# Second gathers during the last expert pass, and rows of the last pass chosen on TensorE, in a fused transformer block

## The reference

```
t = rmsnorm(h)                           # 1024 tokens x 256
probs = softmax(t @ gate_w)              # 8 experts
topw, topi = top_k(probs, 2), topw /= sum(topw)
out_e(t) = (relu(t @ w1[e]) * (t @ w3[e])) @ w2[e]      # hidden width 1024
y = h + sum over the two chosen experts of topw * out_e(t)
result = x + gb * y                      # gb: one row of 256 for each batch
```

## Time and profile before

| | |
|---|---|
| three timed runs, us | 1058.65, 1061.76, 1062.86 (median 1061.76) |
| profiled execution, first to last instruction, us | 1063.1 |
| PE busy | 965.1 us (91%) |
| DVE busy | 789.4 us (74%) |
| ACT busy | 753.5 us (71%) |
| POOL busy | 466.7 us (44%) |
| mean granted TensorE clock | 0.962 |

### The profile page before, as it was taken

The page is one execution under the profiler, slowest core; times in us unless marked ns, Lnnn a source line. Parts: engine busy times, 40 slices in busy tenths (PEclk is TensorE's granted clock), DMA queues, the critical chain, the costliest instruction groups (busy, mean ns, idle before and its releaser), DMA issues.

```text
span 1063.1 us, 22951 instructions
## 1 busy us (share of the span) xinstructions
PE 965.1 (91%) x6862; PEld 901.5 (85%) x6862; DVE 789.4 (74%) x2308; ACT 753.5 (71%) x2122; POOL 466.7 (44%) x550
## 2 busy tenths in 40 slices
PE   5589999999899899999999999999998589999991
PEld 3379899998789799988999999999887489999991
DVE  6779998989899577777777777777764756666646
ACT  3368788887888688788888778877884346555641
POOL 4346668777656333433444332232222852222243
PEclk8899999999999899999999999999997699999996
DMA  8799879787476675465557455354303365555313
GB/s 178 185 233 274 208 190 276 209 213 201 112 177 147 167 190 155 122 164 135 136 140 166 122 168 120 110 153 126 71 1 120 115 221 172 166 170 162 103 58 116
DMA packets 146059, 166.18 MB, mean 156 GB/s; under 512 B 79194, under 2 KB 100714, under 8 KB 140816
## 3 DMA queue, kind: packets, MB, share of 16 engines
q1 hardware_dynamic: 129440, 143.58, 52.0%
q0 software_dynamic: 3712, 11.16, 3.3%
q10 hardware_dynamic: 12784, 9.97, 3.0%
HBM read 105.88 MB, written 58.79 MB: 155 GB/s over the span
## 4 chain that ended last, share of the span: by engine, by line
PE 56%; DVE 17%; issue 10%; ACT 9%; DMA 4%; POOL 1%; SPq 1%; DVEq 0%; ACTq 0%; POOLq 0%
PE psO L1086 14%; PE psS L1053 10%; PE psX L1063 8%; PE psY L1102 6%; PE psP L985 6%; ACT wgt_hi L1319 3%; DVE pbuf L1734 2%; DVE gated L2074 2%; DVE pTl L1756 2%; PE psO L1069 2%; PE psS L1236 2%; PE psP L998 2%; ACT relu_s L1624 2%; PE psX L1236 1%; DVE den L1748 1%
## 5 line engine op out<-in xcount | busy, mean ns | idle before, releaser
L1351 ACT ACTIVATE pbuf<-pbuf,nmax 128x256 f32<-128x256 f32 (+3 forms) x512 | 264.9, 519 | 45.8 <-DVE nmax L1734 44.7
L1053 PE MATMUL psS<-kT,qE 128*128 128x256 f32 (+3 forms) x1024 | 238.2, 317 | 25.7 <-DVE nmax L1734 24.1
L1734 DVE CUSTOM_DVE_ANT_0 pbuf<-psS,mcau 128x256 f32<-128x256 f32 (+3 forms) x512 | 219.9, 435 | 46.9 <-PE psS L1053 41.0
L1756 DVE TENSOR_TENSOR pTl<-psX,pTh 128x512 fp32r<-128x512 f32 x272 | 187.1, 688 | 73.5 <-ACT pTh L1319 72.9
L1319 ACT ACTIVATE pTh<-psX 128x512 fp32r<-128x512 f32 x272 | 160.7, 591 | 55.7 <-PE psO L1086 39.3
L1053 PEld LDWEIGHTS psS<-kT,qE 128*128 128x128 f32 x1024 | 160.2, 192 | 40.3 <-DVE nmax L1734 33.7
L1086 PE MATMUL psO<-pTh,vpad 128*128 128x256 f32 x1088 | 187.1, 294 | 3.2 <-DVE oS L1762 2.0
L798 POOL TENSOR_TENSOR ol<-oS,oh 128x256 fp32r<-128x256 f32 x128 | 94.8, 741 | 200.7 <-ACT oh L1319 196.2
L1063 PE MATMUL psX<-idn,pbuf 128*128 128x128 f32 x1088 | 162.2, 274 | 3.1 <-DVE pTl L1756 3.1
L1086 PEld LDWEIGHTS psO<-pTh,vpad 128*128 128x128 f32 x1088 | 150.3, 190 | 10.5 <-DVE oS L1762 5.4
L1063 PEld LDWEIGHTS psX<-idn,pbuf 128*128 128x128 f32 x1088 | 126.5, 141 | 9.4 <-DVE pTl L1756 3.3
(11 more groups left out here) (295 smaller groups left out, 2369.0 us busy)
## 6 DMA issues: line engine op xcount, KB each, us to landing
qd<-st SPq DMA_DIRECT2D x32, 1024.0 KB, 4.5
qE<-qd SPq DMA_DIRECT2D x128, 256.0 KB, 6.0
mrawV<-in_w_moe SPq DMA_DIRECT2D x32, 384.0 KB
mrawB<-in_w_moe SPq DMA_DIRECT2D x32, 384.0 KB
kT<-kd SPq DMA_DIRECT2D x64, 128.0 KB, 4.4
kT<-kd SPq DMA_DIRECT2D x32, 256.0 KB, 4.3
kd<-st SPq DMA_DIRECT2D x7, 1024.0 KB, 4.8
xg<-sq ACTq DMA_DIRECT2D x7, 640.0 KB, 6.1
```

The costliest lines, as they stand in the source:

```text
L1053: last = mm(psS[j % 2][:, 0:n], qE[:, g % 2, j, t * P:(t + 1) * P], kT[:, g % 2, c, k0:k0 + n], start=(c == 0), stop=(c == 1))
L1351: nc.scalar.activation(pj, pj, ACT.Exp, bias=nmax[:, u % 4, j:j + 1], scale=-1.0, accum_out=sums[:, u % 4, j:j + 1]).then_inc(a_exp, 1)
L1734: V.tensor_tensor_reduce(probs(u, j), psS[j % 2][:, 0:n], mcau[:, SEQ - n:], -SCALE, 3e38, ALU.add, ALU.min, nmax[:, u % 4, j:j + 1]).then ...
L1756: V.tensor_tensor(pTl[:, kt % 2, :], psX[kt % 2][:, :], pTh[:, kt % 2, :], ALU.subtract).then_inc(v_pl, 1)
```

## The change

- The second gathers follow the first ones at once, without waiting for the last pass; the first ones no longer wait for m_gate. A row of `yg` that belongs to the last pass is still zero then. The last pass's output isn't stored to DRAM any more.
- Instead, the last output is kept in SBUF, split in `yh` and `yl`, and for each pair of token tiles TensorE multiplies it with `chooser`, a matrix of zeros and ones of 3 x 128 slots by 1024 tokens: 12 matmuls of 256 columns a pair, 48 in all.
- `chooser` is made by ACT in the last pass, in chunks 1 to 6: relu(1 - (slot - row)^2), two activations of 512 columns a piece, from the tokens' higher slots spread over all partitions. Those come through DRAM: SP stores them (1024 values of 4 bytes, behind the loads of expert 1) and loads them back, spread, ahead of the last pass.
- DVE works out `known` = x part + first rows times share and gate in chunks 4 to 7 of the last pass. POOL works out gate times yN, xN plus that, and `scale2` = gate times second share, two tiles at the start of each of experts 2 to 5.
- Tail: per pair of tiles DVE adds product and second rows, multiplies by `scale2`, and adds `known` for pairs 0 and 2; POOL does that add for pairs 1 and 3. SP stores pairs.
- The last load of `xin` goes from POOL to SP; the flags of `shares` go to tiles of their own (`lesser`, `part`), so that `order` stays.

```diff
@@ -711,6 +738,10 @@
                 if e == 1:
                     sp.wait_ge(s_x, 1)
                 load_expert(e, range(NPC))
+                if e == 1:
+                    sp.wait_ge(v_slot, 2)
+                    sp.dma_start(second_slots.rearrange("(t p) -> p t", p=P), order[:, 1, :],
+                                 allow_slow_non_contiguous=True).then_inc(st_slot, 16)
 
             def leave(i):
...
@@ -719,12 +750,25 @@
                     .then_inc(st_z, 16)
                 sp.dma_start(yg[bass.ds(i * TP + 2 * P, TP - 2 * P), :], ysb[XT * P - TP:P, 2, :]).then_inc(st_z, 16)
 
-            experts(sp, lambda e, first: None, lambda e, i, j, ahead: leave(i), range(NE - 1, NE))
-            leave(first_pass_of(sp, NE))
-            for t in range(NT):
-                sp.wait_ge(v_out, t + 1)
-                sp.dma_start(out[t // TB, t % TB * P:(t % TB + 1) * P, :], xN[:, t, :]).then_inc(st_res, 16)
-            sp.wait_ge(st_res, 16 * NT)
+            def leave_and_load(e, i, j, ahead):
+                leave(i)
+                sp.wait_ge(s_x, i + 2)
+                sp.dma_start(xin[:, :, :], xg[bass.ds((i + 2) * TP, XT * P), :].rearrange("(j p) d -> p j d", p=P))\
+                    .then_inc(st_slot, 16)
+
+            def load_slots(e, first):
+                sp.wait_ge(st_slot, 16)
+                sp.wait_ge(w_hi, NPC * first + NPC - 1)
+                sp.wait_ge(w_lo, 6 * first + 6)
+                sp.dma_start(slot_rows, second_slots.partition_broadcast(P)).then_inc(ld_slot, 16)
+
+            experts(sp, load_slots, leave_and_load, range(NE - 1, NE))
+            for n in range(NT // 2):
+                sp.wait_ge(g_out, n // 2 + 1) if n % 2 else sp.wait_ge(v_out, n // 2 + 1)
+                at = n % 2 * 2 * P
+                sp.dma_start(out[n // 2, at:at + 2 * P, :].rearrange("(t p) d -> p t d", p=P), xN[:, 2 * n:2 * n + 2, :])\
+                    .then_inc(st_res, 16)
+            sp.wait_ge(st_res, 16 * NT // 2)
 
...
+            def begin(e, first):
+                apart(pool)
+                if e == 2:
+                    pool.wait_ge(v_share, 1)
+                    pool.wait_ge(v_ye, 4 * TB)
+                if 2 <= e < 2 + NT // 2:
+                    for t in (2 * e - 4, 2 * e - 3):
+                        link(G.tensor_tensor(yN[:, t, :], yN[:, t, :], GB[:, t // TB, :], ALU.mult))
+                        link(G.tensor_tensor(xN[:, t, :], xN[:, t, :], yN[:, t, :], ALU.add))
+                        link(G.tensor_scalar(scale2[:, t, :], GB[:, t // TB, :], share[:, 1, t:t + 1], None, ALU.mult))
+
+            experts(pool, begin, results, range(NE - 1))
 
             pool.wait_ge(v_slot, 2)
             for i in range(2):
@@ -933,17 +988,18 @@
                     pool.wait_ge(st_y, 32 * first + 16)
                     pool.wait_ge(st_z, 48)
                 else:
-                    experts(pool, lambda e, first: apart(pool), tokens, range(NE - 1, NE))
-                    pool.wait_ge(st_z, 32 * last_passes_of(pool) + 48)
+                    pool.wait_ge(st_z, 32 * last_passes_of(pool) + 16)
                 apart(pool)
                 for t in range(NT):
                     n = i * NT + t
-                    if i == 0:
-                        pool.wait_ge(m_gate, NF * first + t + 1)
-                        apart(pool)
                     G.indirect_dma_start(rows_of(t) if i == 0 else second[:, t, :], None, yg[:, :],
                                          bass.IndirectOffsetOnAxis(ap=slots_out[:, n:n + 1], axis=0))\
                      .then_inc(ld_g[i][t], 16)
+            for n in range(1, NT // 2, 2):
+                pool.wait_ge(v_ready, n // 2 + 1)
+                apart(pool)
+                G.tensor_tensor(xN[:, 2 * n:2 * n + 2, :], second[:, 2 * n:2 * n + 2, :], known[:, 2 * n:2 * n + 2, :], ALU.add)\
+                 .then_inc(g_out, 1)
 
...
             turn_output(first_pass_of(pe, NE))
+            pe.wait_ge(a_choose, 2 * XT * last_passes_of(pe))
+            for n in range(NT // 2):
+                into = (psU + psGt)[n]
+                made = 0
+                for low, js, ready in ((0, (0, 1), 1), (0, (2,), 2), (1, (0, 1), 1), (1, (2,), 2)):
+                    if n == 0:
+                        pe.wait_ge(v_yl if low else a_yh, ready)
+                    for t in range(2):
+                        at = (2 * n + t) * P
+                        for j in js:
+                            last = mm(into[:, t * D:(t + 1) * D], chooser[:, j, at:at + P], (yl if low else yh)[:, j, :],
+                                      start=(made == 0), stop=(made == 4 * XT - 1), skip_group_check=True)
+                            made += 1
+                last.then_inc(s_fin, 1)
 
 
...
 
+            def choose(j, piece):
+
+                k, half = divmod(piece, 2)
+                at = slice(half * SEQ, (half + 1) * SEQ)
+                if piece == 0:
+                    act.wait_ge(ld_slot, 16)
+                nc.scalar.activation(apart2, slot_rows[:, at], ACT.Square, bias=minus[:, k:k + 1]).then_inc(a_apart, 1)
+                act.wait_ge(a_apart, 2 * XT * j + piece + 1)
+                nc.scalar.activation(chooser[:, k, at], apart2, ACT.Relu, bias=ones[:, 0:1], scale=-1.0).then_inc(a_choose, 1)
+
             def one(e, i, j, ahead):
...
                     if e + 1 < NE and f < NF - 1:
                         split_hi(e + 1, f)
+                    if e == NE - 1 and 1 <= f < 1 + 2 * XT:
+                        choose(j, f - 1)
                 tokens_hi(i + 1)
...
             output(tiles)
-            store(tiles, first_pass_of(act, NE - 1), last_passes_of(act))
-            act.wait_ge(ld_xg, 16 * (tiles + 1))
+            act.wait_ge(s_yt, tiles + 1)
+            copy(yh[:, 0:2, :], psTr[0][:, :].rearrange("p (j d) -> p j d", d=D)).then_inc(a_yh, 1)
+            copy(yh[:, 2, :], psTr[1][:, 0:D]).then_inc(a_yh, 1)
+            first, many = first_pass_of(act, NE - 1), last_passes_of(act)
+            act.wait_ge(ld_xg, 16 * first + 16)
+            act.wait_ge(st_slot, 16 * many + 16)
             apart(act)
 
...
             link(V.tensor_copy(boundp, bound))
+            dve.wait_ge(ld_before, 16)
+            link(V.tensor_reduce(rowsum[:, :], before_s[:, :], mybir.AxisListType.X, ALU.add))
+            for j in range(XT):
+                V.tensor_scalar(rowat[:, j:j + 1], rowsum[:, :], -1.0, float(P - 1 + min(j * P, TP - P) - TP), ALU.mult, ALU.add)
             best(range(TB, NT))
...
             link(V.tensor_copy(base_i[:, :], bases))
+            link(V.scalar_tensor_tensor(minus[:, :], bases[:, NE:NE + 1].broadcast_to([P, XT]), -float(TP), rowat[:, :],
+                                        ALU.mult, ALU.subtract))
+            link(V.memset(minus[0:XT * P - TP, XT - 1:XT], 65536.0))
             link(V.scalar_tensor_tensor(based, bases[:, 0:NE].unsqueeze(1).broadcast_to([P, NT, NE]), float(TP),
...
                         split_lo(e + 1, f, NPC * i + NPC)
+                    if e == NE - 1 and f >= NF - NT // 2:
+                        for t in (2 * (f - NF) + NT, 2 * (f - NF) + NT + 1):
+                            dve.wait_ge(ld_g[0][t], 16)
+                            V.scalar_tensor_tensor(known[:, t, :], rows_of(t), share[:, 0, t:t + 1], GB[:, t // TB, :],
+                                                   ALU.mult, ALU.mult).then_inc(v_known, 1)
+                        for t in (2 * (f - NF) + NT, 2 * (f - NF) + NT + 1):
+                            dve.wait_ge(v_known, 2 * NT * j + 2 * (2 * (f - NF) + NT) + t % 2 + 1)
+                            V.tensor_tensor(known[:, t, :], known[:, t, :], xN[:, t, :], ALU.add).then_inc(v_known, 1)
                 tokens_lo(i + 1)
 
...
             output(tiles)
-            store(tiles, first_pass_of(dve, NE - 1), last_passes_of(dve))
-
-
-            for t in range(NT):
-                dve.wait_ge(ld_g[0][t], 16)
-                link(V.scalar_tensor_tensor(yN[:, t, :], rows_of(t), share[:, 0, t:t + 1], yN[:, t, :], ALU.mult, ALU.add))
-            for t in range(NT):
-                b = t // TB
-                dve.wait_ge(ld_g[1][t], 16)
-                link(V.scalar_tensor_tensor(yN[:, t, :], second[:, t, :], share[:, 1, t:t + 1], yN[:, t, :], ALU.mult, ALU.add))
-                link(V.tensor_tensor(yN[:, t, :], yN[:, t, :], GB[:, b, :], ALU.mult))
-                V.tensor_tensor(xN[:, t, :], xN[:, t, :], yN[:, t, :], ALU.add).then_inc(v_out, 1)
+            dve.wait_ge(a_yh, 1)
+            V.tensor_tensor(yl[:, 0:2, :], psTr[0][:, :].rearrange("p (j d) -> p j d", d=D), yh[:, 0:2, :], ALU.subtract).then_inc(v_yl, 1)
+            dve.wait_ge(a_yh, 2)
+            V.tensor_tensor(yl[:, 2, :], psTr[1][:, 0:D], yh[:, 2, :], ALU.subtract).then_inc(v_yl, 1)
+            dve.wait_ge(v_known, 2 * NT * last_passes_of(dve))
+            for n in range(NT // 2):
+                two = slice(2 * n, 2 * n + 2)
+                for t in (2 * n, 2 * n + 1):
```

(8 more changed lines are left out.)

50 lines of the change are left out of this document (41 added, 9 removed).

## The result

The changed kernel takes 1067.81 us (median of four runs, 1066.88 to 1071.89), the kernel before 1060.59 (four runs, 1058.65 to 1062.86). The ratio is 1.0082 with a 95% interval from 1.0065 to 1.01: slower by 0.8%, some 8.7 us (the two medians, of four runs each, differ by 7.2). I had forecast 1060.7 with a range up to 1065.5, so both the time and the sign are wrong.

A forecast was written before the change was run, and what follows sets the result against it. Bound: in loaded passes the ACT-DVE loop, as long as TensorE's 18 matmuls (2.64 us a chunk), then a tail of about 24 us. Tail -4.7, POOL between passes +3.2, routing +0.4: -1.1, from 1061.76 to 1060.7; range 1055 to 1065.5.

The forecast's parts named there:

- in front of the loads of expert 2 they can cost something if the queue is slow with them, at most a few tenths: Small store of the chooser's positions behind expert 1's loads: at most a few tenths of a us, counted as nothing.
- POOL's last add at 1055.65, the store 2.15 later: 1057.8: End of the tail: the last store behind POOL's add of pair 3 ends the span, 5.3 us earlier than before.
- Part 1, the tail: Last pass and tail: store and gather wait go, choosing products and known operations come; gain 4.7 us, between 5.3 and 4.1.
- The last pass: Chunks 4 to 7: DVE's known operations make chunks 2.98 instead of 2.64, so the output's copy starts 2.0 us late.
- cost at nothing: ACT's six chooser pieces: 2.55 a chunk, hidden under TensorE's 2.64; if a piece costs 0.1 more, each chunk loses that.
- Part 2, POOL between passes: Passes of experts 2 to 5: DVE waits for POOL's six operations, two waits of 0.38 a pass; 3.2 us lost, bounds 0 and 6.0.
- the loop has no slack: The 2.64 us loop of DVE and ACT in loaded passes: any DVE delay is carried to the end of the pass.
- some 2 us late: The yg store queued behind POOL's six operations goes out that late; its buffer is wanted a pass later, cost nothing.
- Part 3, routing: Routing: two linked operations of about 0.2 us come into the chain; 0.4 us lost, bound 0 to 0.5.
- The rivals: Four alternatives to the forecast: 1054.7 (chance 0.25, with cases between), 1069.5 (0.07), 1063.9 (0.08), gathers remain the bound (0.02).
- B: Rival: DVE shut out repeatedly by POOL's operations at the start of experts 2 to 5; +7.7 us, 1069.5; chance 0.07.
- D: Rival: the change works as said but the gathers remain the bound, needing issue 4.8 us later; chance 0.02.

The follow-up runs named there:

- e0: The kernel before, unchanged, run again for a second trace: 1060.16 us, span 1058.6.
- e9: The kernel before plus only the small store (1024 values of 4 bytes, behind expert 1's loads, read by nobody): 1066.49 us, ratio 1.005.
- e4: The changed kernel with all last adds on DVE and the 4-byte store issued behind the last expert's weight loads: 1058.83 us, ratio 0.9998 to the kernel before.
- e2: The changed kernel with the slots stored as 128 rows of 32 bytes, read by ACT in strides: 1065.76 us, ratio 1.0049 to the kernel before.
- e3: The changed kernel with both the adds of e1 and the 32-byte store of e2: 1063.51 us, ratio 1.0029 to the kernel before.
- e7: e6 with the known rows of tiles 6 and 7 worked out behind the copy of the output: 1055.67 us, ratio 0.9967 to the kernel before.
- e5: e4 without POOL's six operations at the start of experts 2 to 5 (not the whole computation): 1057.48 us, ratio 0.9972 to the kernel before.
- e6: e4 with the chooser made by DVE in chunks 1 to 3 instead of by ACT: 1058.3 us, ratio 0.9985 to the kernel before.
- e1: The changed kernel with the last adds of pairs 1 and 3 on DVE instead of POOL: 1062.87 us, ratio 1.0025 to the kernel before.
- e10: e7 with filler matmuls, three ahead of the turned output and four behind it: 1057.24 us, ratio 0.9969 to the kernel before.

## Why the prediction was wrong

By stages, the changed kernel against e0, with the forecast behind it: ahead of pass 0 +1.2 (+0.4), pass 0 to 1 +3.9 (nothing, at most a few tenths), passes 1 to 7 +1.2 (+3.2), from there to the end -0.4 (-4.7). In the last one 3.2 are POOL's part of the tail and 2.0 the half clock, of which 0.6 had been counted.

**The step that failed most: "in front of the loads of expert 2 they can cost something if the queue is slow with them, at most a few tenths".** By e9 it is the largest cost of the change, 5.3 us alone. I had asked when the values are needed (150 us later) and not what stands beside them: POOL's scatters of the token rows are in flight at that time, and pass 1 needs them. Shown is that with the 4-byte store at that place POOL waits 8.2 to 10.5 us for the scatters (three traces) where it otherwise waits 2.6 to 4.2 (ten traces), and that 32-byte rows or a later place take that away. The bytes are the same in both forms, so it is the number and size of the packets that decide. It isn't the scatters alone: stores beside the same small store at its later place (e4) land 6 us later as well. That the small packets hold up others because all share the 16 DMA engines is how I read it (share 1.10 at 123 GB/s); what happens in the queues was not measured.

**The second: "POOL's last add at 1055.65, the store 2.15 later: 1057.8".** I took the end from the store, as in the kernel before, where DVE adds last. With POOL adding last, its drain ends 4.9 to 5.0 behind its last operation, and SP is through with the stores 2.0 to 2.4 behind it. What POOL does in that time is not shown. The row was there to be read in the trace of before, among the records of L156:

```profile
L156 POOLq DRAIN  x1: 11958/11958/11958, 1049.6 to 1049.6; - x1
```

That drain ends at 1061.56, 5.0 behind POOL's last gather (1055.52 and 1.01 in the earlier trace rows) and 1.5 ahead of the end. I had never asked when POOL itself may stop. By the traces it costs 2.6 to 3.0, and with the slower adds and DVE's wait for one of them (L2214, 1.26 instead of 0.69) the POOL part of the tail costs 3.2 (20.19 against 16.99; e2 against e3 gives 4.0, of which 0.9 is the clock: 5.33 against 4.46 for the first 24 products).

How the 0.82% divides between these two can be told less well than their sum. From the changed kernel to e4 both go, 0.0084 or 8.9 us. Taken first, the adds give 6.0 and the store's place 2.9; e2, which takes the store first, gives 3.5 and 3.0 more that its strided read ate, and the adds 2.1 after it (e3). In the original kernel they cost: the store 5.3, one add on POOL 2.4. Each ratio has an interval of 1.5 to 2.2 us to either side, and a difference of two of them more.

**Part 1, the tail: right but for POOL's end.** From the copy to the end I had 22.5 down to 15.2 at full clock. With all adds on DVE it is 14.95 and 15.01 (e4, e7). From the start of the turned output to the end of the last store I had 14.6; e4 has 14.1 (1043.57 to SP's drain at 1057.7), e7 14.1 too, the changed kernel 16.8 at half clock. The gathers were no bound, as said. Half clock costs what I gave it, 1.2, where the turning is still at full clock and the first 24 products at 0.61 to 0.65 (15.90 to 16.17 in e3, e5 and e6 against 14.95 in e4: 1.0 to 1.2), and more where it is down from the turning on (16.99 in e1, whose turning has 0.62 and first products 0.51: 2.0).

**The last pass: 2.0 late forecast, 1.7 measured, with the shares exchanged.** DVE's chunks are 2.90 apart, not 2.98, since the four known operations take 1.46 (1034.17 to 1035.63), not 1.54. The copy is 2.67 behind the last low part, not 3.2: of the 1.23 that I took from the earlier trace rows for the two token operations they use 0.80 (1044.31 to 1045.11), the rest had been idle time. In return ACT's pieces, "cost at nothing", cost what I had put beside it as a warning: the activations took 0.71 and 0.72, not 0.63, and chunks 1 to 3 became 2.80.

**Part 2, POOL between passes: 3.2 forecast, 1.0 to 1.2 measured** (0.29 a pass, where I had 0.8; the passes are 23.84, not 24.0 or more). The waits are there, 0.21 and 0.34 in the low parts, of the size of my 0.38 from the earlier trace rows; the subtractions, for which I had up to 1.7, keep their 0.96. What failed is "the loop has no slack": the wait falls on the low part, behind which DVE was idle for ACT's rounding, and the row of 1000.20 in the earlier trace rows shows that idle time (0.24). The 0.29 comes later and elsewhere, at chunk 4. I had also put the stores to `yg` "some 2 us late" and priced that at nothing; they are 4.9 late, and go out right ahead of the one rounding that comes late. The Trainium skill (SBUF — State Buffer, Who interferes with whom) has the two engines shut each other out for a whole instruction; the trace agrees for the low parts, which end 0.35 behind POOL's operation each time (904.52 behind 904.17, 907.77 behind 907.42). It doesn't for the subtraction of 905.04, which has two SBUF operands too, overlaps POOL's tensor_scalar (until 905.32) by 0.28 and takes its usual 0.96.

**Part 3, routing: 0.4 forecast.** Mark to pass 0 is 33.3 to 34.3 in four traces of the old routing and 32.7 to 36.5 in nine of the new, 34.6 in the changed kernel's own: the stage as a whole can't tell. The two new operations can be read in DVE's timeline of the changed kernel: they start at 830.80 and 831.02, and the next one at 831.11, so they put 0.31 into the chain.

**The rivals.** None happened. B has the right sign and nearly the right size, 1069.5, but by luck: DVE's waits, its reason, are worth 1.2 and not 12. D's question, whether something other than the products ends the kernel, was the right one, asked of the gathers only.

**What stays open.** From the mark to the end e4 is 4.3 us shorter than e0, by the timed runs 0.2 (interval: 1.9 shorter to 1.6 longer). The whole spans differ by 0.7 only, since e4's mark stands 3.6 later; if the changed kernels were longer ahead of the mark as well, the table would hide it (marks 814.0 to 817.7 in nine traces with the change, 813.6 to 815.7 in four without). Half clock in the first products, which e1, e3, e5 and e6 show and e4, e7 and e10 don't, is worth 1 to 2 us of that if most timed runs have it; the rest is not explained, nor why the clock falls in one execution and not in the next. What holds ACT's rounding in chunk 3 of passes 2 to 5 is open too: a store to `yg` that goes out earlier, with the six operations kept, would tell.

## What to carry to other kernels

A small transfer is not judged by when its data is needed but by what is in flight when it goes out: a store of single 4-byte values is moved to where nobody waits for a DMA. And the last store is not always the end: ask of the last instruction of each engine how long that engine then needs to stop, and keep the final operation off POOL when its drain is the longer way out. Before a wait is priced, follow it one instruction further, since the next one may have been idle for something else.
